# Scaling a softmax mixer on ScalarE instead of VectorE, in a gated two-branch network on one core

## The reference

```python
xn = _layernorm(x)
s = _L0_attn_ref(xn, ...)            # 16 heads, with mixing over heads before and after the softmax
g = _silu(_L0_ffn_ref(xn, ...))      # two layers: local attention (window 128) and a gated MLP
x = x + s * g
```

```python
logits = jnp.einsum('bhid,bhjd->bhij', q, k) * SCALE
logits = jnp.einsum('bhij,gh->bgij', logits, Wpre)
attn = jax.nn.softmax(logits, axis=-1)
attn = jnp.einsum('bhij,gh->bgij', attn, Wpost)
```

## Time and profile before

| | |
|---|---|
| median of 3 runs | 5370.03 us (5368.29 to 5371.4) |
| device time of the profiled execution | 5372.07 us |
| its span | 5370.0 us |
| busy: TensorE, VectorE, ScalarE, GpSimd | 5119.1, 3692.1, 2659.8, 2619.2 us |
| mean granted TensorE clock | 0.994 |

### The profile page before, as it was taken

How to read it: one execution, slowest core, us unless ns; L and a number is a source line. 1 busy time by engine, 2 the same in 40 slices (tenths; PEclk the granted TensorE clock), 3 DMA queues, 4 the chain that set the end, 5 groups by cost and what they waited for, 6 DMA issues and landing times. The chain is left out here.

```text
span 5370.0 us, 176617 instructions
## 1 busy us (share of the span) xinstructions
PE 5119.1 (95%) x72856; PEld 4155.2 (77%) x72856; DVE 3692.1 (69%) x8889; ACT 2659.8 (50%) x6551; POOL 2619.2 (49%) x2308
## 2 busy tenths in 40 slices
...
GB/s 79 95 66 63 46 35 64 45 67 42 38 61 56 57 41 38 61 61 53 40 64 35 61 53 51 58 31 61 54 50 58 30 61 62 42 58 39 52 49 17
DMA packets 51388, 280.78 MB, mean 52 GB/s; under 512 B 5280, under 2 KB 22688, under 8 KB 33696
## 3 DMA queue, kind: packets, MB, share of 16 engines
...
## 5 line engine op out<-in xcount | busy, mean ns | idle before, releaser
L1492 POOL TENSOR_TENSOR q_lo<-q_mix,q_hi 128x512 fp32r<-128x512 f32 x512 | 663.5, 1296 | 1349.7 <-ACT q_hi L979 1349.7
L992 ACT ACTIVATE probs<-bank_S,neg_max 128x512 f32<-128x512 f32 x1024 | 700.6, 685 | 1180.3 <-DVE neg_max L1220 993.7
L711 PE MATMUL bank_S<-k_hi,q_lo 128*128 128x512 f32 x2048 | 874.5, 427 | 9.6 <-POOL q_lo L1492 5.5
L1220 DVE TENSOR_REDUCE neg_max<-bank_S 128x1 f32<-128x512 f32 x1024 | 693.8, 684 | 263.5 <-PE bank_S L713 259.7
L713 PE MATMUL bank_S<-k_hi,q_hi 128*128 128x512 f32 x2048 | 803.9, 393 | 0.0
L712 PE MATMUL bank_S<-k_lo,q_hi 128*128 128x512 f32 x2048 | 803.5, 392 | 0.1
L728 PEld LDWEIGHTS bank_M<-mixer_n,probs 64*64 64x64 f32 x32768 | 534.1, 136 | 248.5 <-issue 161.3
L728 PE MATMUL bank_M<-mixer_n,probs 64*64 64x64 f32 x32768 | 606.1, 222 | 74.3 <-DVE mixer_n L1211 24.3
L1518 POOL TENSOR_TENSOR l_probs<-l_probs,l_inv 128x1024 f32<-128x1024 f32 (+1 forms) x256 | 428.8, 1682 | 491.7 <-DVE l_inv L1323 491.7
L1487 POOL TENSOR_TENSOR q_mix<-q_rope,w_pre 128x256 f32<-128x256 f32 x1024 | 637.6, 643 | 48.6 <-POOL q_lo L1492 1.8
L1042 ACT ACTIVATE l_probs<-l_probs,l_least 128x256 f32<-128x256 f32 (+1 forms) x1024 | 480.9, 471 | 253.0 <-DVE l_least L1303 252.6
...
## 6 DMA issues: line engine op xcount, KB each, us to landing
...
```

The source lines that it names most:

```text
L711: mm(bank[k][:], q_lo[q], k_hi[:, s, :], start=(s == 0), stop=False)
L992: fn(probs[:, n % PB, :], bank[k][:], ACT.Exp, bias=neg_max[:, n % 2:n % 2 + 1], accum_out=row_sum[:, n % 4:n % 4 + 1]).then_inc(emptied[k ...
L1220: v.tensor_reduce(neg_max[:, n % 2:n % 2 + 1], bank[k][:], AX.X, ALU.max, negate=True)\
L1492: g.tensor_tensor(q_lo[:, c % QB], q_mix[:], q_hi[:, c % QB].bitcast(F32), ALU.subtract)\
```

## The change

Three things change. The multiplication in "mixers" moves from VectorE to ScalarE, where it is two copies with a scale per partition; VectorE keeps the reciprocal. The addition of 1 in the sigmoid moves from four steps on VectorE to one instruction on ScalarE behind the exponential in "bound". And all three order lists are new, which moves steps on every engine. Two waits go with that: "talk_v" now waits for the turned x itself, since it may stand ahead of "talk_q", and "x_turn" on ScalarE waits for all three talk steps.

```diff
             def scores(step, n):
...
+            def mixers(step, m):
+                act.wait_ge(inv_done, now.at(inv_done, m + 1))
+                if now.past(not (m < 2)):
+                    act.wait_ge(filled["M1"], now.fill(("mix", (m - 2) % PAIRS), "M1", ago=m < 2))
+                for t in range(2):
+                    ins = fn(mixer_n[:, m % 2, t, :], mixer[:].rearrange("p g i -> p (g i)"), ACT.Copy,
+                             scale=row_inv[:, m % 2, t:t + 1])
+                ins.then_inc(mixer_done, 1)
...
             def bound(step):
                 act.wait_ge(bounded, now.at(bounded, 0))
                 fn(x_mid[:], x_mid[:], ACT.Exp, scale=-1.0).then_inc(exp_done, 1)
+                act.wait_ge(exp_done, now.at(exp_done, 0))
+                fn(x_mid[:], x_mid[:], ACT.Identity, bias=1.0).then_inc(one_plus, 1)
...
                 v.reciprocal(row_inv[:, m % 2, :], row_sum[:, m % 2 * 2:m % 2 * 2 + 2]).then_inc(inv_done, 1)
-                if now.past(not (m < 2)):
-                    dve.wait_ge(filled["M1"], now.fill(("mix", (m - 2) % PAIRS), "M1", ago=m < 2))
-                dve.wait_ge(inv_done, now.at(inv_done, m + 1))
-                shape = [P, 2, GH * HI]
-                v.tensor_tensor(mixer_n[:, m % 2], mixer[:].rearrange("p g i -> p (g i)")[:, None, :].to_broadcast(shape),
-                                row_inv[:, m % 2, :, None].to_broadcast(shape), ALU.mult).then_inc(mixer_done, 1)
...
             def sigmoid(step, t):
                 if not t:
-                    dve.wait_ge(exp_done, now.at(exp_done, 0))
-                v.tensor_scalar(x_mid[:, t, :], x_mid[:, t, :], 1.0, None, ALU.add).then_inc(one_plus, 1)
-                dve.wait_ge(one_plus, now.at(one_plus, t + 1 - TW))
+                    dve.wait_ge(one_plus, now.at(one_plus, 0))
                 v.reciprocal(x_mid[:, t, :], x_mid[:, t, :]).then_inc(sig_done, 1)
```

One line each of the order lists (of `ORDER`, the stretch with the last two sigmoids):

```diff
-mixers.6 scores.14 scores.15 mix.6 weigh.0.3 p_turn.0.1 sigmoid.2 part.9 silu scores.16 gated sigmoid.3 mixers.7
+part.9 scores.14 weigh.0.2 expand.10 scores.15 silu local_values.0.1 local_scores.0.3 mix.6 mixers.7 sigmoid.2 gated
```

More of the change, by code:

```diff
@@ L124 @@
 ORDER = """
[L125 to L129, removed]
@@ L135 @@
[L135 to L139, removed]
@@ L140 @@
[L140 to L154, removed]
@@ L155 @@
-down.1.2 talk_v values.7 down.1.3 project.3
+expand.0 part.0 expand.1 part.1 expand.2 qkv.0.0 scores.0 join.0.0 scores.1 part.2 expand.3 qkv.0.1 mixers.0 part.3
+q_turn.0.0 expand.4 k_turn.0.0 bound join.0.1 scores.2 scores.3 part.4 mix.0 qkv.0.2 mixers.1 k_turn.0.1 expand.5
+scores.4 q_turn.0.1 scores.5 join.0.2 part.5 mix.1 qkv.0.3 mixers.2 k_turn.0.2 scores.6 expand.6 scores.7 mix.2
+mixers.3 q_turn.0.2 join.0.3 scores.8 mix.3 part.6 expand.7 sigmoid.0 q_turn.0.3 scores.9 k_turn.0.3 values.0
@@ new lines @@
+sigmoid.1 part.7 mixers.4 local_scores.0.0 scores.10 scores.11 expand.8 weigh.0.0 mix.4 mixers.5 part.8 expand.9
+local_scores.0.1 scores.12 p_turn.0.0 weigh.0.1 scores.13 mix.5 local_scores.0.2 local_values.0.0 p_turn.0.1 mixers.6
+part.9 scores.14 weigh.0.2 expand.10 scores.15 silu local_values.0.1 local_scores.0.3 mix.6 mixers.7 sigmoid.2 gated
+scores.16 weigh.0.3 sigmoid.3 store p_turn.0.2 scores.17 mix.7 local_scores.0.4 mixers.8 part.10 out_proj.0.0
+expand.11 scores.18 values.1 local_values.0.2 weigh.0.4 local_scores.0.5 p_turn.0.3 scores.19 part.11 mix.8
@@ L162 @@
[L162 to L186, removed]
@@ L187 @@
[L187 to L189 removed]
+expand.0 part.0 expand.1 part.1 sigmoid.0 expand.2 qkv.0.0 join.0.0 part.2 expand.3 scores.0 scores.1 qkv.0.1 scores.2
+join.0.1 k_turn.0.0 q_turn.0.0 part.3 mixers.0 qkv.0.2 mix.0 expand.4 scores.3 scores.4 join.0.2 mixers.1 part.4
@@ new lines @@
+q_turn.0.1 expand.5 k_turn.0.1 qkv.0.3 mix.1 scores.5 scores.6 k_turn.0.2 mixers.2 join.0.3 part.5 q_turn.0.2 scores.7
+mix.2 q_turn.0.3 k_turn.0.3 expand.6 mixers.3 scores.8 part.6 local_scores.0.0 mix.3 weigh.0.0 scores.9 scores.10
+expand.7 part.7 local_scores.0.1 mixers.4 p_turn.0.0 weigh.0.1 values.0 expand.8 local_scores.0.2 scores.11 mix.4
+weigh.0.2 mixers.5 scores.12 p_turn.0.1 local_values.0.0 part.8 local_scores.0.3 mix.5 expand.9 scores.13 p_turn.0.2
+local_values.0.1 weigh.0.3 local_scores.0.4 scores.14 weigh.0.4 out_proj.0.0 part.9 local_values.0.2 p_turn.0.3
@@ new lines @@
+mixers.6 local_scores.0.5 local_values.0.3 expand.10 part.10 p_turn.0.4 scores.15 local_scores.0.6 mix.6 weigh.0.5
+weigh.0.6 out_proj.0.1 mixers.7 scores.16 local_values.0.4 p_turn.0.5 mix.7 expand.11 local_scores.0.7
+local_values.0.5 p_turn.0.6 weigh.0.7 scores.17 scores.18 part.11 out_proj.0.2 expand.12 local_values.0.6 p_turn.0.7
+part.12 values.1 expand.13 mixers.8 local_values.0.7 scores.19 out_proj.0.3 mix.8 half_turn.0 mixers.9 scores.20
+shift_turn.0 part.13 scores.21 scores.22 expand.14 mix.9 mixers.10 h_scale.0 sigmoid.1 scores.23 scores.24 mixers.11
@@ new lines @@
+scores.48 mixers.23 scores.49 out_proj.1.0 expand.27 mix.23 local_scores.1.5 local_values.1.2 p_turn.1.3 mixers.24
+scores.50 values.5 weigh.1.4 local_values.1.3 local_scores.1.6 weigh.1.5 mix.24 p_turn.1.4 silu part.27 weigh.1.6
+scores.51 mixers.25 scores.52 out_proj.1.1 bound local_values.1.4 p_turn.1.5 mix.25 local_scores.1.7 local_values.1.5
+p_turn.1.6 weigh.1.7 scores.53 mixers.26 scores.54 expand.28 out_proj.1.2 local_values.1.6 p_turn.1.7 mix.26 scores.55
+part.28 expand.29 local_values.1.7 mixers.27 part.29 project.2 expand.30 out_proj.1.3 mix.27 half_turn.1 scores.56
@@ L190 @@
+shift_turn.1 part.30 scores.57 scores.58 values.6 expand.31 sigmoid.3 store mixers.28 h_scale.1 part.31 scores.59
+mix.28 mixers.29 gated scores.60 h_turn.1 mix.29 scores.61 mixers.30 scores.62 norm up.1.0 up.1.1 scores.63 scale
+mixers.31 mix.30 up.1.2 up.1.3 mix.31 up.1.4 values.7 x_turn.0 project.3 up.1.5 talk_q down.1.0 talk_k down.1.1
+down.1.2 down.1.3 talk_v
 """
 LAST_ORDER = """
-expand.0 part.0 expand.1 part.1 expand.2 bound qkv.0.0 scores.0 part.2 join.0.0 expand.3 scores.1 qkv.0.1 part.3
@@ L199 @@
-mixers.6 p_turn.0.1 weigh.0.2 part.9 weigh.0.3 scores.15 sigmoid.2 expand.10 mix.6 silu mixers.7 scores.16 sigmoid.3
-gated part.10 p_turn.0.2 local_values.0.1 local_scores.0.4 scores.17 scores.18 out_proj.0.0 mix.7 expand.11
-local_scores.0.5 weigh.0.4 p_turn.0.3 local_values.0.2 values.1 part.11 mixers.8 weigh.0.5 local_scores.0.6
-local_values.0.3 p_turn.0.4 scores.19 weigh.0.6 expand.12 mix.8 local_scores.0.7 store mixers.9 out_proj.0.1 part.12
-local_values.0.4 weigh.0.7 p_turn.0.5 mix.9 p_turn.0.6 local_values.0.5 scores.20 expand.13 out_proj.0.2
@@ L219 @@
-out_proj.1.2 local_values.1.6 p_turn.1.7 scores.53 part.29 local_values.1.7 scores.54 scores.55 expand.30 mixers.26
-out_proj.1.3 mix.26 half_turn.1 part.30 expand.31 mixers.27 scores.56 mix.27 shift_turn.1 scores.57 scores.58
-mixers.28 values.6 part.31 h_scale.1 scores.59 scores.60 mix.28 mixers.29 end.silu h_turn.1 scores.61 scores.62
-mixers.30 mix.29 up.1.0 up.1.1 up.1.2 up.1.3 up.1.4 up.1.5 scores.63 mix.30 down.1.0 down.1.1 down.1.2 mixers.31
-down.1.3 end.bound mix.31 end.gated end.sigmoid.0 end.sigmoid.1 end.sigmoid.2 end.sigmoid.3 values.7 project.3
@@ L224 @@
-end.store
+expand.0 part.0 expand.1 part.1 qkv.0.0 join.0.0 scores.0 expand.2 scores.1 qkv.0.1 join.0.1 q_turn.0.0 mixers.0
+part.2 expand.3 k_turn.0.0 qkv.0.2 mix.0 scores.2 scores.3 join.0.2 part.3 k_turn.0.1 q_turn.0.1 expand.4 scores.4
+mixers.1 q_turn.0.2 bound k_turn.0.2 qkv.0.3 part.4 expand.5 scores.5 join.0.3 mix.1 mixers.2 scores.6 scores.7 part.5
+sigmoid.0 mixers.3 mix.2 expand.6 q_turn.0.3 part.6 scores.8 k_turn.0.3 sigmoid.1 local_scores.0.0 mix.3 scores.9
+weigh.0.0 scores.10 mixers.4 local_scores.0.1 values.0 sigmoid.2 expand.7 scores.11 p_turn.0.0 part.7 mix.4 expand.8
```

96 lines of the change are left out of this document (65 added, 31 removed).

## The result

The changed kernel takes 5209.24 us in the median of 4 runs (5208.23 to 5209.67), against 5370.72 us for the kernel before: a ratio of 0.970, 95% interval 0.9683 to 0.9716. That is 161 us faster. The direction was right, the size was not.

The account below looks back on a forecast made before the run. TensorE, busy 5119.1 of 5370.0 us, was taken as the bound, idling mostly for late VectorE. 5372.07 - 98 (waits) - 16 (clock) + 10 + 10 (new waits) - 1 (end) = 5277, so 5275 us against the median; range 5210 to 5350.

Parts of the forecast that it names:

- what comes back and what stays: New waits on TensorE from the new order, 10 us and 10 us, and waits for GpSimd and ScalarE that stay.
- (a): mix.3 and mix.27, with only 3.0 us of matmuls after their last scores, wait 0.3 us each: 10 us.
- (b): Layer 1: ScalarE's 6.5 us per pair of scores overhangs TensorE's about 6 us, costing 0.6 us a batch: 10 us.
- (c): Steps without late VectorE ahead keep their waits: k_turn.1.0 for GpSimd, 18.2 us; values for a ScalarE copy, 14.9 us.
- What goes for VectorE: TensorE's waits for late VectorE: 85.6 us go whole, half of 13.0 and 11.8 us too: 98 us.
- more goes: Rival: all waits for VectorE, GpSimd and ScalarE go with the clock loss, nothing returns: 5210 us, chance 0.14.
- 16 us of low clock: TensorE's lower clock in the 7 us from out_proj.0.0 on, after 3 us of idling, costs 16 us, which goes.
- The reading with two SBUF inputs: VectorE instructions with two SBUF inputs share a read port with GpSimd; mixers' multiplication loses 200 us to stretch.
- its own sign of being wrong: Prediction is wrong if a new place waits over 1 us in every batch, above all for ScalarE's probs or mixer_n.
- The scaled copy: mixers on ScalarE: 1024 copies of 128x64 at 0.30 us each, 0.60 a pair, 307 us in all.
- that rival: New stretches of other VectorE instructions and a worse order offset the gain: 5370 us, chance 0.05.
- Slower: Rival: mixers on ScalarE waits for VectorE's queued reciprocal, decisive from 0.22 us per pair; 5410 us at 0.3; chance 0.10.

Follow-up runs that it names:

- e8: Changed kernel, each scaled copy on ScalarE also writing an unused accumulated sum: 5220.55 us, ratio 0.9711 to the kernel before.
- e9: Kernel before, with one place of ORDER rearranged (local_values.0.1 and scores.16 ahead of sigmoid.2 and sigmoid.3): 5358.66 us, ratio 0.9963.
- e2: New lists and added waits, with the multiplication and the addition of 1 on VectorE as in the kernel before: 5240.15 us, ratio 0.9754 to it.
- e3: Kernel before, old order, mixers' multiplication on VectorE as two tensor_scalar with an unused accumulated sum: 5269.1 us, ratio 0.9803.

## Why the prediction was wrong

The four corners say it best: before 5371; moves alone 5285 (-88 beside its own runs of before); lists alone 5240 (-132); both 5209 (-161). The two gains overlap: 88 + 132 = 220.

- **The new order, mis-sized and of the wrong sign.** The step that failed is the one on what comes back and what stays. It charged (a) 10 us for two tight mixes, (b) 10 us for ScalarE's overhang in layer 1, and (c) let the waits for GpSimd and ScalarE stand. In the trace after no steady row for mixer_n is left (3.2 us, once), the 18.2 us are 0.9 and the 14.9 us are gone. Of (a), mix.27 is tight but fits: with 0.17 us more a pair in e8 it waits 0.15 us a batch, and mix.3 doesn't wait even then. (b) doesn't show at all: the rows after the change have no wait for ScalarE that comes more than once, in layer 1 or elsewhere. The lists did not only keep the waits from coming back; alone they were worth 132 us.
- **What goes for VectorE.** Predicted 98 of 110.4 us; all 110.4 went, the half that was left for join and the bank copies too. The steps named the rival "more goes" for this, with 5210 us: that is what happened, at a chance of 0.14.
- **The sum by parts.** Idle time -133.7 us, of it 110.4 + 17.3 + 14.9 = 142.6 from those rows, less 25.3 + 8.3 = 33.6 us for the two new waits (neither foreseen). Busy time -29.3 us, of it 16 us of low clock as predicted; the other 13 us lie inside groups of matmuls and are not traced to a cause. The idle rows leave 142.6 - 33.6 = 109 us of the 133.7. Most of the other 25 us is in four places: the two rows "issue" for mix and values (17.3 + 16.6 us before, 9.9 + 13.9 after), VectorE's `mixed` before the turns of L787 (6.6, now 0.3), ScalarE's `probs` before scores (4.2, now 1.0), and the time behind the last matmul (15.4, now 10.8 us, where the prediction had 1 us).
- **The clock.** The 16 us came as predicted, but that they hang on the 3 us of idling is not shown. In the changed kernel both are gone; e9 has no such idle time either, and a mean clock of 0.991; e2 has none over 2.0 us in its steady part, and 0.994. That all 16 us went is in part luck.
- **The mechanism.** Right for the waits, and shown by e3: the stretched multiplication made them in the old order, 103 us. Of the 187 multiplications of over 400 ns in the trace before, 185 end 0.15 us after a GpSimd instruction that had started first. The reading with two SBUF inputs was too narrow: of the two stretched instructions that the prediction shows, the addition of 1 has one. That the moves alone gave 88 us and the form alone 103 is a sign of what ScalarE costs in that order: its copies came late 68 times.
- **The signs.** No row for mixer_n on VectorE, the clock of 1.00 behind out_proj.0.0 and ScalarE at 2933.1 us came as said. Waits for VectorE under 30 us did not: 25.3 + 8.3 + 1.2 = 34.8 us without the first input. And its own sign of being wrong came up, though not for ScalarE: a new place, talk_v, waits 1.7 us in 15 batches.
- **The scaled copy.** 0.34 us, where the sum had 0.30; 299 us in all against 307, since neighbours overlap. By the Trainium skill, "ScalarE: Activation LUTs", section "What ACT_TABLE_LOAD costs", the estimate for this shape is 332 ns; the trace has 331 to 366. None of the 1024 is stretched, beside a GpSimd as busy as before (2614.3 us).
- **VectorE near 3300 us.** It is 3371.8. The stretch did move on, as that rival said, but to a place where nobody waits: the new order has GpSimd's rotation of q beside VectorE's rotation of k. The cast of k, shortest, median and longest:

```profile
L1198 DVE CAST k_hi<-k_rope x16: 694/2728/2730, 51.4 to 4866.1; 128x1024 fp32r<-128x1024 f32 x16
...
who waited for it (us, times):
```

Some 2 us of stretch in one instruction with one SBUF source, and the list of who waited for it is empty.

- **Slower.** The 0.22 us per pair did not come; TensorE waited for mixer_n once.

Open are the 13 us of busy time, and which words of the three lists carry the 132 us; e9 shows only that one place does not.
